# A two-layer transformer block on one core: 16-bit score planes, and the weights' scaling moved from GpSimd to ScalarE

## The reference

```python
x = x + L0_xattn(layernorm(x), ctx)      # fake-quantised product: q1 @ q2
x = x + L0_ffn(layernorm(x))             # x @ W.T + b, plus a routed low-rank part
x = x + L1_xattn(layernorm(x), ctx)      # the attention below
x = x + L1_ffn(layernorm(x))             # x @ W_up, plus a top-1 low-rank part
# L1_xattn: 32 query heads, 8 key/value heads, head size 128
q = rope(query @ wq); k = rope(ctx @ wk); v = ctx @ wv
raw = einsum('bhqd,bhkd->bhqk', q, k) / sqrt(128) + mask
out = softmax(raw) @ v;  result = out @ wo
```

## Time and profile before

| | |
|---|---|
| runs shown | 2067.95, 2069.71, 2070.38 us |
| profiled execution, its own time | 2063.38 us |
| its span, first to last instruction | 2061.6 us |
| mean granted TensorE clock | 0.992 |
| TensorE (PE) busy | 2001.8 us, 97% |
| weight loads (PEld) busy | 1235.3 us, 60% |
| VectorE (DVE) busy | 1599.0 us, 78% |
| ScalarE (ACT) busy | 1080.4 us, 52% |
| GpSimd (POOL) busy | 1266.2 us, 61% |
| chain that ended last | PE 77%, DVE 6%, DMA 3%, issue 2%, ACT 2%, POOL 2% |

### The profile page before, as it was taken

One profiled execution on the slowest core, in us unless ns is written; L12 is line 12 of the kernel. 1 busy time (PEld: TensorE's weight loads), 2 busy tenths in 40 slices (PEclk: granted clock), 3 DMA queues, 4 the chain that ended last, 5 costly groups with the idle time before them and its releaser, 6 DMA issues.

```text
span 2061.6 us, 26211 instructions
## 1 busy us (share of the span) xinstructions
PE 2001.8 (97%) x9118; PEld 1235.3 (60%) x9122; DVE 1599.0 (78%) x2903; ACT 1080.4 (52%) x1674; POOL 1266.2 (61%) x751
## 2 busy tenths in 40 slices
PE   8999999999889999999999999999999999999899
PEld 6877786877645555555555555555555555555487
DVE  5776776676678888888888888888888888888743
ACT  3443353336466566565655656566565656656400
POOL 1552352422167788887778877777777778875500
PEclk9999999999999999999999999999999999999999
DMA  7663675455998787887778899887787887877612
GB/s 267 225 208 118 210 242 174 164 178 170 311 214 175 160 172 146 182 174 164 169 159 172 174 217 215 214 172 174 153 174 166 165 188 144 168 161 144 193 62 72
DMA packets 673379, 366.32 MB, mean 178 GB/s; under 512 B 576768, under 2 KB 593408, under 8 KB 671200
## 3 DMA queue, kind: packets, MB, share of 16 engines
q1 hardware_dynamic: 673248, 364.65, 72.1%
HBM read 182.12 MB, written 39.85 MB: 108 GB/s over the span
## 4 chain that ended last, share of the span: by engine, by line
PE 77%; DVE 6%; DMA 3%; issue 2%; ACT 2%; POOL 2%; SPq 0%; ACTq 0%; DVEq 0%; POOLq 0%
PE ps L43 25%; PE ps L45 24%; PE ps L44 24%; PE ps L876 1%; POOL u_sb L2134 1%; DMA pT<-pp 1%; DVE t_sb L1239 1%; DMA raw<-in_ctx 1%; DVE pp L1658 1%; DVE psb L1641 0%; DVE vhl_sb L1311 0%; ACT wh L1797 0%; DVE u_sb L1239 0%; PE ps L1133 0%; PE ps L883 0%
## 5 line engine op out<-in xcount | busy, mean ns | idle before, releaser
L2175 POOL TENSOR_SCALAR araw<-araw,sc 128x512 f32<-128x512 f32 x256 | 563.2, 2200 | 51.9 <-DMA araw<-in_wq 51.9
L1658 DVE SCALAR_TENSOR_TENSOR pp<-psb,st,pp 128x1024 f16<-128x1024 f32 x256 | 400.3, 1564 | 3.5 <-ACT pp L2027 1.5
L2020 ACT ACTIVATE psb<-psb,st 128x1024 f32<-128x1024 f32 x256 | 294.7, 1151 | 195.7 <-DVE st L1644 195.7
L2027 ACT ACTIVATE pp<-psb,st 128x1024 f16<-128x1024 f32 x256 | 294.4, 1150 | 159.7 <-DVE st L1653 154.5
L1641 DVE CUSTOM_DVE_ANT_0 psb<-ps,mask 128x1024 f32<-128x1024 f32 x256 | 313.4, 1224 | 70.4 <-PE ps L45 67.5
L43 PE MATMUL ps<-ksb,qsb 128*128 128x512 f32 x512 | 250.8, 490 | 9.5 <-DVE st L1641 6.9
L2181 POOL TENSOR_TENSOR wol<-araw,woh 128x512 f16<-128x512 f32 x128 | 149.0, 1165 | 109.4 <-ACT woh L1953 109.4
L43 PE MATMUL ps<-woh,osb 128*128 128x512 f16 x512 | 195.0, 381 | 9.2 <-issue 4.8
L45 PE MATMUL ps<-ksb,qsb 128*128 128x512 f32 x512 | 203.0, 396 | 0.0
L44 PE MATMUL ps<-ksb,qsb 128*128 128x512 f32 x512 | 202.6, 396 | 0.0
L1674 DVE SCALAR_TENSOR_TENSOR x_lo<-ps,sc,x_lo 128x512 f32<-128x512 f32 x256 | 190.4, 744 | 14.0 <-PE ps L45 12.8
(11 more groups left out here) (283 smaller groups left out, 3981.4 us busy)
## 6 DMA issues: line engine op xcount, KB each, us to landing
araw<-in_wq SPq DMA_DIRECT2D x128, 256.0 KB, 4.7
araw<-in_wo SPq DMA_DIRECT2D x128, 256.0 KB, 4.3
k_scratch<-khl SPq DMA_DIRECT2D x32, 512.0 KB, 3.6
scan<-in_wq SPq DMA_DIRECT2D x64, 256.0 KB, 4.9
scan<-in_wo SPq DMA_DIRECT2D x64, 256.0 KB, 4.7
ksb<-k_scratch SPq DMA_DIRECT2D x16, 1024.0 KB, 6.1
raw<-in_wv SPq DMA_DIRECT2D x16, 512.0 KB, 5.0
raw<-in_ctxT SPq DMA_DIRECT2D x16, 512.0 KB, 4.5
```

The source lines that it names most:

```text
L1658: e.scalar_tensor_tensor(out=pp[:, r, 1024:2048], in0=psb[:, r, :], scalar=st[:, n // 4 % 4, 16 + i:17 + i], in1=pp[:, r, 0:1024], op0=ALU ...
L2020: e.activation(P, P, ACT.Exp, bias=c[:, 4 + i:5 + i], accum_out=c[:, 8 + i:9 + i]).then_inc(a_exp.sem, 1)
L2027: e.activation(pp[:, r, 0:1024], psb[:, r, :], ACT.Copy, scale=st[:, n // 4 % 4, 16 + i:17 + i]).then_inc(a_ph.sem, 1)
L2175: e.tensor_scalar(w_raw(n), w_raw(n), sc[:, 16 + wo:17 + wo], None, ALU.mult).then_inc(p_ws.sem, 1)
```

## The change

1. Key and query planes (`khl`, `k_scratch`, `ksb`, `qsb`) become float16 instead of float32r. To keep their size in range, keys are scaled. Each of the eight key slices and each batch's context gets a power of two from its sum of squares: ScalarE sums squares of c0 to c15 and of the eight key slices w1, w3, ... w15 (`key_square`, 24 operations of 128x1024), TensorE sums over partitions (`key_squares`, nine small matmuls with `twos`, each behind a key or value step), VectorE makes the scales (`context_squares`, `key_scale`, five tiny operations each). The rotation of keys takes the scale as a further factor.
2. The scores come out scaled. The mask is multiplied by the same scale on VectorE (`scale_mask`, 128x1024, four tiles for each batch), the negative maximum and the exponent take the inverse as a factor in their operations. The scaling of `cosq` and `sinq` on VectorE goes; a constant factor is in the tables as given. `query_scale` has more tiny operations.
3. The slices of wq and wo are scaled on ScalarE (`split_w`), in place, right before the cast, which waits for it; GpSimd's `scale_w` goes. ScalarE waits for the slice's DMA itself. For wq the scale is one for each key head.

Unused allocations keep the addresses as they were; the scratch of dynamic DMAs is smaller. The diff, cut:

```diff
-    k_d = nc.dram_tensor("k_scratch", [16, 128, 2, 1024], F32, kind="Internal").ap()
+    k_d = nc.dram_tensor("k_scratch", [16, 128, 2, 1024], F16, kind="Internal").ap()
...
-    khl = alloc(one, "khl", [128, 2, 2, 512], F32R)
+    khl = alloc(one, "khl", [128, 2, 2, 512], F16)
+    junk = alloc(one, "junk", [128, 1024], BF16)
...
-    ksb = alloc(two, "ksb", [128, 2, 2, 1024], F32R)
+    ksb = alloc(two, "ksb", [128, 2, 2, 1024], F16)
...
-    qsb = alloc(two, "qsb", [128, 2, 2, 512], F32R)
+    qsb = alloc(two, "qsb", [128, 2, 2, 512], F16)
...
+    KEY_SUM_AT = {0: 0, 5: 1, 9: 2, 13: 3, 17: 4, 20: 5, 25: 6, 29: 7, 32: "c1"}
...
+        def key_squares(key):
+
+            if key == 0:
+                e.wait_ge(v_scal.sem, v_scal[0])
+            elif key == "c1":
+                e.wait_ge(v_kc.sem, v_kc[7, 0])
+            else:
+                e.wait_ge(v_kc.sem, v_kc[key - 1, 0])
+            if key == 5:
+                e.wait_ge(a_a1T.sem, a_a1T[2])
+            if key == 6:
+                e.wait_ge(v_l0.sem, v_l0[0, 7, 0])
+            if key in (0, "c1"):
+                e.wait_ge(v_cq.sem, v_cq[1 if key else 0])
+            if key != "c1":
+                e.wait_ge(a_kq.sem, a_kq[key])
+            a, z = (1, 3) if key == 0 else (0, 1) if key == "c1" else (2 + key, 3 + key)
+            e.matmul(ps[:, 7 if key == 5 else 4, a:z], twos[:, :], ksq[:, 16 + a:16 + z], start=True, stop=True).then_inc(
+                t_kc.sem, 1)
...
+            if s in KEY_SUM_AT:
+                key_squares(KEY_SUM_AT[s])
...
+        def scaled_rope(src, scale, cos, sin, u, t):
+            e.scalar_tensor_tensor(out=u, in0=src, scalar=scale, in1=cos, op0=ALU.mult, op1=ALU.mult)
+            e.scalar_tensor_tensor(out=t[0:64], in0=src[64:128], scalar=scale[64:128], in1=sin[64:128], op0=ALU.mult,
+                                   op1=ALU.mult)
+            return e.scalar_tensor_tensor(out=t[64:128], in0=src[0:64], scalar=scale[0:64], in1=sin[0:64], op0=ALU.mult,
+                                          op1=ALU.mult)
+
+        def half_exponents(dst, src):
+
+            return e.tensor_scalar(dst.bitcast(I32), src.bitcast(I32), 0x7F000000, 1, ALU.bitwise_and, ALU.logical_shift_right)
+
+        def context_squares(b):
+            e.wait_ge(a_kq.sem, a_kq["c", 8 * b + 7])
+            e.tensor_reduce(ksq[:, 17 - b:18 - b], ksq[:, 8 * b:8 * b + 8], AX, ALU.add).then_inc(v_cq.sem, 1)
+
+        def key_scale(key):
+
+
+            a, z = (1, 3) if key == 0 else (0, 1) if key == "c1" else (2 + key, 3 + key)
+            e.wait_ge(t_kc.sem, t_kc[key])
+            e.tensor_scalar(kst[:, a:z], ps[:, 7 if key == 5 else 4, a:z], 2.0 ** -60, 2.0 ** 60, ALU.max,
+                            ALU.min).then_inc(v_kc.sem, 1)
+            e.wait_ge(v_kc.sem, v_kc[key, 0])
+            half_exponents(kst[:, 10 + a:10 + z], kst[:, a:z]).then_inc(v_kc.sem, 1)
+            e.wait_ge(v_kc.sem, v_kc[key, 1])
+            e.tensor_scalar(kst[:, 10 + a:10 + z], kst[:, 10 + a:10 + z], 2.0 ** 63, None, ALU.mult).then_inc(v_kc.sem, 1)
+            e.wait_ge(v_kc.sem, v_kc[key, 2])
+            e.reciprocal(kst[:, 20 + a:20 + z], kst[:, 10 + a:10 + z]).then_inc(v_kc.sem, 1)
+            e.wait_ge(v_kc.sem, v_kc[key, 3])
+            if key == "c1":
+                e.tensor_scalar(ksc[:, 8:16], kst[:, 22:30], kst[:, 20:21], 2.0 ** 12, ALU.mult, ALU.mult).then_inc(v_kc.sem, 1)
+            else:
+                e.tensor_scalar(ksc[:, key:key + 1], kst[:, 22 + key:23 + key], kst[:, 21:22], 2.0 ** 12, ALU.mult,
+                                ALU.mult).then_inc(v_kc.sem, 1)
...
-            rope(bank(KV_BANKS[s % 5]), cosk[:, cs], sink[:, cs], u_sb[:, o, :], t_sb[:, :]).then_inc(v_kr.sem, 1)
+            scaled_rope(bank(KV_BANKS[s % 5]), ksc[:, s // 4:s // 4 + 1], cosk[:, cs], sink[:, cs], u_sb[:, o, :],
+                        t_sb[:, :]).then_inc(v_kr.sem, 1)
...
-            floor_roots(1, "w", 2)
-            e.tensor_scalar(sc[:, 16:17], sc[:, 12:13], 2.0 ** 14, None, ALU.mult).then_inc(v_ws.sem, 1)
-            e.tensor_scalar(sc[:, 18:19], sc[:, 9:10], 2.0 ** -14 / H_SCALE, None, ALU.mult).then_inc(v_ws.sem, 1)
+
+            floor_roots(2, "w", 3)
+            e.tensor_scalar(sc[:, 16:17], sc[:, 12:13], sc[:, 13:14], 2.0 ** 14, ALU.mult, ALU.mult).then_inc(v_ws.sem, 1)
+            e.tensor_scalar(sc[:, 18:19], sc[:, 9:10], sc[:, 10:11], 2.0 ** -24, ALU.mult, ALU.mult).then_inc(v_ws.sem, 1)
+            e.wait_ge(v_ws.sem, v_ws["w", 7])
+            e.tensor_scalar(kst[:, 30:38], kst[:, 12:20], sc[:, 16:17], None, ALU.mult).then_inc(v_ws.sem, 1)
+            e.wait_ge(v_ws.sem, v_ws["w", 8])
+            e.tensor_scalar(sc[:, 22:24], kst[:, 10:12], sc[:, 18:19], None, ALU.mult).then_inc(v_ws.sem, 1)
+            e.wait_ge(v_ws.sem, v_ws["w", 9])
+            e.reciprocal(kst[:, 38:40], sc[:, 22:24]).then_inc(v_ws.sem, 1)
...
+                context_squares(s // 32)
                 kv_end(s)
                 kv_end(s + 1)
+                key_scale(KEY_SUM_AT[s])
...
-                e.tensor_scalar(cosq[:, :], cosq[:, :], sc[:, 18:19], None, ALU.mult).then_inc(v_ws.sem, 1)
-                e.tensor_scalar(sinq[:, :], sinq[:, :], sc[:, 18:19], None, ALU.mult).then_inc(v_ws.sem, 1)
-                e.wait_ge(v_ws.sem, v_ws["sinq"])
...
+        def scale_mask(b, i):
+            e.wait_ge(d_m[i].sem, d_m[i][b])
+            e.tensor_scalar(mask[:, i, :], mask[:, i, :], kst[:, 39 - b:40 - b], LOWEST, ALU.mult, ALU.max).then_inc(v_m.sem, 1)
...
-            e.tensor_scalar(c[:, 4 + i:5 + i], c[:, i:i + 1], -1.0, None, ALU.mult).then_inc(v_nmax.sem, 1)
+            e.tensor_scalar(c[:, 4 + i:5 + i], c[:, i:i + 1], sc[:, 23 - H // 32:24 - H // 32], -1.0, ALU.mult,
+                            ALU.mult).then_inc(v_nmax.sem, 1)
...
         q_end(0, 7)
+        scale_mask(0, 0)
         q_end(1, 6)
+        scale_mask(0, 1)
         scores_max(0)
         h_lo(7)
         row_scale(0)
         scores_max(1)
         p_lo(0)
         row_scale(1)
+        scale_mask(0, 2)
         scores_max(2)
+        scale_mask(0, 3)
...
+        def key_square(key):
+
+            n = 2 * key + 1 if key in range(8) else key[1]
+            name, at = (f"w{n}", 18 + key) if key in range(8) else (f"c{n}", n)
+            e.wait_ge(a_hi.sem, a_hi[name])
+            if key != ("c", 0):
+                e.wait_ge(a_kq.sem, a_kq[key] - 1)
+            e.activation(junk[:, :], f32(split_dst(name, 0)), ACT.Square, accum_out=ksq[:, at:at + 1]).then_inc(a_kq.sem, 1)
+
         for key in SPLIT_ORDER[:10]:
             split_hi(key)
+            if key in ("c5", "c6", "c7"):
+                key_square(("c", int(key[1:]) - 5))
+        for c in range(3, 8):
+            key_square(("c", c))
+        key_square(0)
...
-            e.wait_ge(p_ws.sem, p_ws[n])
+            wo, r, G = key[0] == "o", W_SLOT[n], key[1] // 8 % 8
+            e.wait_ge(d_ar[r].sem, d_ar[r][n])
+            if n == 0:
+                e.wait_ge(v_ws.sem, v_ws["w", 9])
+            if wo and n < 12:
+                e.wait_ge(v_ws.sem, v_ws["v", 8])
+            scale = sc[:, 17:18] if wo else kst[:, 30 + G:31 + G]
+            e.activation(w_raw(n), w_raw(n), ACT.Copy, scale=scale).then_inc(a_ws.sem, 1)
...
+            e.wait_ge(a_ws.sem, a_ws[n])
             e.copy(w_dst(key, 0), w_raw(n)).then_inc(a_whi.sem, 1)
...
-            e.activation(P, P, ACT.Exp, bias=c[:, 4 + i:5 + i], accum_out=c[:, 8 + i:9 + i]).then_inc(a_exp.sem, 1)
+            e.activation(P, P, ACT.Exp, bias=c[:, 4 + i:5 + i], scale=sc[:, 23 - H // 32:24 - H // 32], accum_out=c[:, 8 + i:9 + i]).then_inc(a_exp.sem, 1)
...
-        def scale_w(n):
-            if n < len(W_ORDER):
-                wo, r = W_ORDER[n][0] == "o", W_SLOT[n]
-                e.wait_ge(d_ar[r].sem, d_ar[r][n])
-                if n == 0:
-                    e.wait_ge(v_ws.sem, v_ws["w", 5])
-                if wo and n < 12:
-                    e.wait_ge(v_ws.sem, v_ws["v", 8])
-                e.tensor_scalar(w_raw(n), w_raw(n), sc[:, 16 + wo:17 + wo], None, ALU.mult).then_inc(p_ws.sem, 1)
-
         def split_w(key):
             n = W_AT[key]
-            scale_w(n + 1)
             e.wait_ge(a_whi.sem, a_whi[n])
             e.tensor_tensor(w_dst(key, 1), w_raw(n), w_dst(key, 0), ALU.subtract).then_inc(p_wlo.sem, 1)
...
-    cosq = (np.concatenate([cos, cos], 0)[:, :512] / root).astype(np.float32)
-    sinq = (np.concatenate([sin, -sin], 0)[:, :512] / root).astype(np.float32)
+    cosq = (np.concatenate([cos, cos], 0)[:, :512] / root * 2.0 ** -12).astype(np.float32)
+    sinq = (np.concatenate([sin, -sin], 0)[:, :512] / root * 2.0 ** -12).astype(np.float32)
```

More of the change, by code:

```diff
@@ L423, in build_in @@
     v_kr = signal("v_kr", KS)
+    v_kc = signal("v_kc", [(key, j) for key in [*range(8), "c1"] for j in range(5)])
+    v_cq = signal("v_cq", range(2))
+    v_m = signal("v_m", [(b, i) for b in range(2) for i in range(4)])
```

55 lines of the change are left out of this document (41 added, 14 removed).

## The result

The change made the kernel slower. The changed kernel: 2083.48 us median of four runs (2082.25 to 2085.6), the kernel before 2068.83 beside it; ratio 1.0081, interval 1.0062 to 1.0099. Forecast were 2053.0 and a range of 2042 to 2068. The profiled execution of the changed kernel took 2082.25 us, 18.9 more than that of before.

A forecast was written before the change was run, and what follows sets the result against it. TensorE was taken to bound the attention loop. Gain 26.3 us less additions 9.7 gives net -16.6, profiled 2063.4 to 2046.8; 6.3 more for the median gives 2053, range 2042 to 2068.

The forecast's parts named there:

- the predicted spacing: Attention loop: a short step of 18 matmuls, all 16-bit, takes TensorE 3.88 to 3.90 us in place of 3.99.
- the third rival: Scores in the loop: the 0.107 us came from switching banks or readers, not the planes; 2079 us; chance 0.04.
- the fourth: Rival: score loads stand outside the matmuls, so shrinking each by 0.09 us gives 138 us; 1941 us; chance 0.01.
- 3.3 + 1.4 + 1 + 0.5 + 2.5: Added us: TensorE's stop at the start, small sums of squares, VectorE's chains and scaled multiplications, query scales, handover.
- The masks at head 32: Four more masks scaled at head 32, 3.2 us of VectorE in four steps: +1 us (0 to 3.2).
- Who waits for that lag?: Attention loop: only the value product, through the transposes, was said to wait for ScalarE's lag; slack 0.68 us holds.
- The slack of the chain that was looked for: Low plane's end to value product: 5.19 - 4.3 = 0.89 us, shrinking by 0.21 to 0.68; lag 0.2 to 0.4.
- VectorE would gain cover: Loop: GpSimd works less beside VectorE's low plane, 1.28 us undisturbed, some 1.56 mean; gives cover and no time.
- The loop of ScalarE and VectorE: High plane to next high plane: 3.23 us, with scaling 0.70 and wait 0.15 about 4.0 to 4.1.
- the second rival: Loop: ScalarE becomes the bound through its pace with VectorE; net gain nil at 4.35 us, 2089 at 4.5; chance 0.08.
- what would show it: Signs of right, such as heads near 20.85 us apart, and of wrong, such as transpose waits over 10 us in the loop.
- the rivals that they belong to: Partly lost: TensorE waits for transposes, 0.15 us a head, 2063, chance 0.12; slower: ScalarE's pace with VectorE bounds, chance 0.08.

The follow-up runs named there:

- experiment 3: The changed kernel with the sum of squares of key slice 5 on TensorE behind step 21 instead of step 20: 2069.92 us, ratio 1.0025.
- Experiments 4: The changed kernel with the output's high plane ahead of the query's on ScalarE, nothing else: 2068.05 us, ratio 1.0018.
- 10: The kernel before with one edit, the output's high plane on ScalarE ahead of the next query's: 2059.31 us, ratio 0.9961.
- 6: The changed kernel, scale kept on ScalarE, with the output's high plane ahead of the query's and the fifth key sum a step later: 2070.74 us, ratio 1.0015.
- 8: The kernel of 6 without the factor in the exponent and the negative maximum, leaving out the head's scale of the scores: 2063.15 us, ratio 0.9975.
- 11: The changed kernel with the scale on GpSimd and the output's high plane ahead of the query's, fifth key sum not moved: 2055.82 us, ratio 0.9942.
- 12: The changed kernel with scale on GpSimd, output's high plane ahead of the query's, fifth key sum a step later; second measurement: 2053.43 us, ratio 0.9927.
- experiment 7: The kernel of 12 with the squares at the start, TensorE's first sums and VectorE's tiny operations reordered: 2057.73 us, ratio 0.9950.

## Why the prediction was wrong

**The gain was there.** In the step the predicted spacing holds: 3.88 us for a short step without a stop, and the scores' 26 to 27 us of the excess over the floor vanished. That the effect is none of the type's (the third rival) is excluded, and so are weight loads in full (the fourth): they lost 119 us of busy time in the loop and gave none of it back. By the rule of the Trainium skill (TensorE: Matmul & The Clock Gate, section The mechanism) they should have; here the trace disagrees, as step and load times show.

**The additions up to the loop were right in their sum, in part by luck.** Forecast 8.7 us up to the attention loop (3.3 + 1.4 + 1 + 0.5 + 2.5); measured 616.9 - 608.5 = 8.3. In the second profiled execution of the same kernel it was 13.7 (622.3). Their parts were not as forecast: the first stop was 1.7 us by its row instead of 3.3 (ScalarE's seven squares began at 24.27, not behind 25.62), and a stop of 4.2 us with a half-clock stretch behind it, in front of key sum 5, was not forecast at all. In experiment 3 its removal was made up for by the next stop. The masks at head 32 were priced at 1 us; heads 28 to 34 took 134.2 us, before 129.8, so 4.4, of which 0.7 is what six other heads got longer by.

**The step that failed is "Who waits for that lag?"**: it overlooked the one chain that had no slack, and at the one it looked at both the slack and the thing that uses it up were wrong.

*The chain that was not looked for.* The prediction named the transposes as the only ones that wait. The output product waits as well, behind VectorE's rotation, GpSimd's addition and the query's cast. It showed in the profile of before: part of those 4.7 us "issue" of the earlier trace rows, which I added up to "7 us" and passed over as small. A small wait that comes back 18 to 20 times is a chain whose slack is zero; all lag goes straight through it. In the heads that stop, VectorE ended the rotation 4.22 us before the output product was due in the kernel before, and 3.78 in the changed one (median of 24): 0.44 later against a TensorE that is faster, and the stop grew from 0.34 to 0.79. With the scale back on GpSimd (experiment 1) it is 3.71 and 0.85, with 32-bit scores and the scale on ScalarE (experiment 2) 4.22 and 0.34, so the length of these stops comes from the 16-bit planes and not from the scale. Experiments 4 and 10 show the chain: without the query's cast in front, the stops vanish in both kernels.

*The slack of the chain that was looked for.* It was 0.89 less 0.21 for two score groups, 0.68. The 0.21 is right: from the deciding maximum on VectorE to the value product the median is 7.78 us over 56 heads before and 7.57 after, stops taken off. But two things were missed. The product needs at least 4.52 us from the low plane's end, not the DMA's 4.3: the chain above has 4.25 for the DMA and 0.35 behind it. And the negative maximum, which stands in front of the low plane, got its factor. In the changed kernel 4.89 us are left behind a low plane of 1.28, so the slack was 0.36 and not 0.68; before it was 5.18 - 4.52 = 0.66.

*What uses it up.* The low plane was taken as 1.28, undisturbed, and I wrote that VectorE would gain cover from a less busy GpSimd. The head's last low plane took 1.37 in the mean before, with none of 56 over 1.9 us; after 1.74, with 28 of 56 over 1.9. In the mean of all low planes nothing changed (1.57 and 1.55). GpSimd does half the work, but its one subtraction now starts when ScalarE's cast ends, and at 1014.78 that is just in front of VectorE's low plane. The Trainium skill (SBUF — State Buffer, section Who interferes with whom) has the two engines share a port pair that one of them holds alone, which the prediction had read as a gain in cover; the trace agrees with the rule, and not with that reading of it. Head by head this accounts for the stops: a low plane of 2.09 is 0.81 longer, less 0.36 of slack makes 0.45, and such heads stop by 0.44 to 0.65. Of heads 3 to 60 all 36 with a last low plane of over 1.75 us stop, and of the 22 with 1.28 only one does, at the new masks. In experiments 4, 6 and 8 it was over 1.9 us in 42, 47 and 46 of 57 heads. With the scale on GpSimd (1, 11 and 12) it was so in at most one, but not short: 1.70 to 1.73 in the mean, beside subtractions and scalings, and these kernels keep 12.6 to 17 us of short stops.

*The lag itself.* The loop of ScalarE and VectorE was priced at 4.0 to 4.1 and measured at 4.13. The scaling is 0.71 (0.70 forecast), from its start to that of the cast 0.79 (0.85 forecast), so that term was right; the factors' 0.15 the sum lacked. But the second rival's mechanism, a lag of 2 x (L - 3.88) at the transposes, is not what stopped TensorE: in 35 of 37 heads with a stop the deciding maximum had waited for TensorE's scores and began 0.04 us behind them, and the high plane was done 0.8 us or more before the low plane began. What ScalarE's new work did there was to move the cast, and with it GpSimd's subtraction, to a place where they hurt. No run moved the subtraction alone.

In sum: for the 62 heads 1330.9 was measured where 1322.4 - 26.5 + 1 = 1296.9 was forecast. Of these 34.0 us, 31 are the growth of the two kinds of stops (9.5 to 40.5): 13.9 before output products, 17.1 before value products. The rest is small; a part of it lies behind the stop of 2.4 us at the new masks, where the granted clock is 0.63 from 1305 to 1309 us (before 1.00 from 1295 to 1305). The part behind the loop took 2 us more, which was priced at nothing. So the profiled execution came 35.4 us above the forecast for it (2082.25 against 2046.8); the median came 30.5 above, as the 6.3 us added for the median were 1.2 this time.

**What of the list "what would show it" held.** Waits for the transposes over 10 us: 14.2 by the waits. ScalarE without idle time before the exponent: 20.6 in place of 185.5. Heads 21.37 apart, not 20.85. The first two were signs named for "wrong", and they came; the rivals that they belong to had 0.20 of the chances, and neither knew the output product or the long low plane.

**What is open.** Why the stops before output products vanish late in the loop in experiment 3 and stay in the changed kernel, though the code there is the same, which is most of that experiment's 11 us; and the 4 us that experiment 7's loop is longer. The loop settles into patterns that depend on how it is entered. That of the changed kernel was seen twice (1330.9, 1332.4), but what selects it was not found.

## What to carry to other kernels

When work is moved to an engine that is not at its bound, don't price the engine but its list: for each instruction behind the moved one, who waits for it, and what stands in front of it that waits for somebody else. In the profile of before, read the idle time in front of the engine's pacing instruction (here the exponent, 185.5 us over 240 steps, 0.77 a step; the move took 0.79, the factors 0.15, and the shorter step of TensorE 0.11) as the budget, and every small wait that recurs as a chain with none. And when a chain's margin is computed, take the durations at that place, count the whole way up to the instruction that waits, and ask what the change moves beside them: a mean over all places hid the 0.81 us by which the low planes that counted got longer.

## What the runs showed of the hardware that was not expected

- A factor read through a pointer is not free on ScalarE at 1024 columns: the exponent takes 1238 ns with it and 1148 without. A 512-wide copy with it takes 0.71 us, the 512-wide cast without it 0.62.
- VectorE's low plane of 128x1024 (three operands, 1.28 undisturbed) takes 1.80 to 2.23 us where a GpSimd subtraction of a wo slice was already running; where the low plane was first it keeps 1.28 and the subtraction takes 1.67 to 1.93 in place of 1.16. So the subtractions of wo slices took 1531 ns in the mean, 1159 before, while those of wq stayed at 1161.
- Halving the storage of scores' operands took 119 us of weight-load time out of the loop, with nothing gained by it.
